# The numerator's state product of a linear-attention layer on half of the contraction rows, in two banks instead of one

## The reference

```python
qkv = x @ W_attn + b_attn                 # 16 heads of 16 channels
q, k = elu(q) + 1, elu(k) + 1
def step(carry, inp):
    kv, ksum = carry                      # per head 16 x 16 and 16
    kv = kv + kt[..., :, None] * vt[..., None, :]
    ksum = ksum + kt
    num = einsum('bhi,bhij->bhj', qt, kv)
    den = einsum('bhi,bhi->bh', qt, ksum)[..., None] + EPS
    return (kv, ksum), num / den
y = y @ W_proj + b_proj
```

## Time and profile before

| | us |
|---|---|
| median of 3 runs | 2399.52 |
| the three runs | 2395.42, 2399.52, 3922.05 |
| profiled execution, its own time | 2388.81 |
| its span, first to last instruction | 2387.1 |
| TensorE busy | 2074.3 |
| VectorE busy | 2055.3 |
| ScalarE busy | 1893.9 |
| GpSimd busy | 1210.0 |

### The profile page before, as it was taken

The page is one execution under the profiler, slowest core; times in us unless marked ns, Lnnn a source line. Parts: engine busy times, 40 slices in busy tenths (PEclk is TensorE's granted clock), DMA queues, the critical chain, the costliest instruction groups (busy, mean ns, idle before and its releaser), DMA issues. The chain is left out here.

```text
span 2387.1 us, 40867 instructions
## 1 busy us (share of the span) xinstructions
PE 2074.3 (87%) x12844; PEld 1296.4 (54%) x12844; DVE 2055.3 (86%) x3876; ACT 1893.9 (79%) x3800; POOL 1210.0 (51%) x1804
## 2 busy tenths in 40 slices
PE   2448898998989899898989989898998989889887
PEld 1115556464655646465565646556564656646574
DVE  7988998979889897989989798998979899897734
ACT  5779887897978789797878979787897978867453
POOL 7114454545545454554546455454645555464744
PEclk8669899999999999999999999999999999999999
DMA  3542422323132232313223232322223132221000
GB/s 84 134 113 54 107 56 66 83 60 92 47 105 56 70 79 63 89 47 104 56 71 79 65 87 50 102 56 75 75 66 85 52 100 56 70 70 34 5 6 12
DMA packets 104452, 165.98 MB, mean 70 GB/s; under 512 B 15459, under 2 KB 34095, under 8 KB 104239
## 3 DMA queue, kind: packets, MB, share of 16 engines
q1 hardware_dynamic: 104238, 163.37, 25.7%
HBM read 146.55 MB, written 16.78 MB: 68 GB/s over the span
## 5 line engine op out<-in xcount | busy, mean ns | idle before, releaser
L1399 DVE TENSOR_TENSOR_SCAN scan_bufs<-scan_bufs,inp_bank 128x512 f32<-128x512 f32 x512 | 617.8, 1207 | 4.9 <-ACT scan_bufs L794 4.4
L1108 PE MATMUL bank<-w_gu,f_xqT 128*128 128x512 f32 x1024 | 496.6, 630 | 36.3 <-ACT f_xqT L857 35.1
L787 ACT ACTIVATE scan_bufs<-scan_bufs,a_rows 128x512 f32<-128x512 f32 x512 | 371.5, 725 | 54.8 <-DMA scan_bufs<-dt_copy 54.5
L1123 PE MATMUL bank<-w_dn,f_hqT 128*128 128x256 f32 x1536 | 357.9, 383 | 8.6 <-ACT f_hqT L857 8.6
L1108 PEld LDWEIGHTS bank<-w_gu,f_xqT 128*128 128x128 f32 x1024 | 201.1, 202 | 269.1 <-issue 265.0
L1409 DVE TENSOR_TENSOR scan_bufs<-scan_bufs,c_bank 128x512 f32<-128x512 f32 x512 | 343.1, 670 | 1.2
L794 ACT ACTIVATE scan_bufs<-scan_bufs 128x512 f32<-128x512 f32 x512 | 323.6, 632 | 3.9
L1123 PEld LDWEIGHTS bank<-w_dn,f_hqT 128*128 128x128 f32 x1536 | 284.3, 190 | 77.3 <-issue 26.0
L688 POOL TENSOR_TENSOR f_h<-f_h,f_h_scale 128x704 f32<-128x704 f32 x128 | 178.1, 1391 | 283.8 <-DVE f_h L1274 283.8
L710 POOL TENSOR_SCALAR_AFFINE_SELECT masked_scores<-masked_scores 128x512 f32<-128x512 f32 x256 | 168.8, 685 | 217.1 <-ACT masked_scores L857 216.8
L699 POOL TENSOR_TENSOR f_h<-f_h,f_h_lean 128x704 f32<-128x704 f32 x128 | 216.1, 1688 | 122.2 <-DVE f_h L1460 113.1
(11 more groups left out here) (196 smaller groups left out, 4408.3 us busy)
## 6 DMA issues: line engine op xcount, KB each, us to landing
scan_bufs<-dt_copy SPq DMA_DIRECT2D x512, 256.0 KB, 4.1
xp<-L_attn_a_x SPq DMA_DIRECT2D x16, 512.0 KB, 4.1
dt_copy<-dt SPq DMA_DIRECT2D x32, 256.0 KB, 2.8
out<-x SPq DMA_DIRECT2D x64, 128.0 KB, 3.5
w_attn<-L_attn_b_W_attn SPq DMA_DIRECT2D x1, 768.0 KB, 4.9
masked_scores<-L_ffn_w_gate SPq DMA_DIRECT2D x1, 704.0 KB
masked_scores<-L_ffn_w_up SPq DMA_DIRECT2D x1, 704.0 KB
f_h<-L_ffn_w_down SPq DMA_DIRECT2D x2, 352.0 KB, 11.1
```

Of the source, the lines that this page charges most:

```text
L787: nc.scalar.activation(half, half, ACT.Exp, scale=a_rows[:, c, at:at + 1]).then_inc(root_ready, 1)
L1108: last = nc.tensor.matmul(to[:, :], f.xqT[:, k, :], w_gu[:, k, g, lo:hi], start=(k == 0), stop=(k == DH - 1))
L1123: last = nc.tensor.matmul(to[:, 0:D], f.hqT[:, k, :], w_dn[:, k, :], start=(k == 0), stop=(k == FK - 1))
L1399: nc.vector.tensor_tensor_scan(half, half, inp[:, :], 0.0, ALU.mult, ALU.add)\
```

## The change

The state product is split by contraction rows. Of a head group of 128 rows the first 64 rows are the four heads of an even set, the last 64 those of an odd set. Each product now uses only the 64 rows of its own heads, of kv and of q. Even and odd products write different banks, uses "num0" and "num1", in each of which only 256 of 512 columns are used (one 128-column piece per head group). The products with the masked scores go to the same places; order and count of all products stay. Each bank gets its own filled signal: num0 after set 2, num1 after set 3. ScalarE copies each with an instruction of its own, 128x256, to sets 0 and 2 or 1 and 3 of numT. a_flip waits for both copies; the exponential of q and k two tiles on waits for num1. VectorE waits for the drain of use "B" before it makes inp. The tables HEAD, LAST_AT and LAST_SHIFT are rewritten as plain lists, GAPS and SHIFT; TIMES and PARTS_AT stay.

```diff
-                  ... "num": ("a_sum", "act", "a_sum"),
+                  ... "num0": ("a_sum", "act", "a_sum"),
+                  "num1": ("a_sum", "act", "a_sum"),
...
 def beat_of(engine, part, step, t, b):
-    at = start_of(engine, part, step, t)
-    if b == NB - 1 and part in LAST_AT:
-        first, gap = LAST_AT[part]
-        at += first - PARTS_AT[part][0] + t * (gap - PARTS_AT[part][1])
-        at += LAST_SHIFT.get(engine, {}).get((part, step), 0.0)
+    at = start_of(engine, part, step, t) + t * GAPS.get((b, part), 0.0)
+    at += SHIFT.get(b, {}).get(engine, {}).get((part, step), 0.0)
...
 (ScalarE, a_root)
-                        wait_drained(act, "R1", b if t > 1 else b - 1, (t - 2) % TILES, "num")
+                        wait_drained(act, "R1", b if t > 1 else b - 1, (t - 2) % TILES, "num1")
 (ScalarE, a_sum)
-                    copy_out(f1, b, t, "num", numT[:, :, :].rearrange("p s n -> p (s n)"), SETS * P)
+                    for e in range(2):
+                        src, done = wait_filled(act, "R1", b, t, f"num{e}")
+                        nc.scalar.activation(numT[:, :, :].rearrange("p (g e) n -> p e g n", e=2)[:, e, :, :],
+                                             src[:, 0:2 * P].rearrange("p (g n) -> p g n", g=DH), ACT.Copy)\
+                            .then_inc(done, 1)
 (TensorE, a_sum)
-                    to, filled = take("R1", b, t, "num", ["v"])
+                    taken = [take("R1", b, t, f"num{e}", ["v"]) for e in range(2)]
                     if t:
-                        for st in range(SETS):
-                            grp, lo = divmod(4 * st, HG)
-                            nc.tensor.matmul(to[:, st * P:(st + 1) * P],
-                                             kv[:, grp, lo:lo + 4, :].rearrange("p h j -> p (h j)"),
-                                             fqk[r][:, 0, grp, :], start=(st == 0), stop=False,
-                                             skip_group_check=True)
+                        for grp in range(DH):
+                            for e in range(2):
+                                rows = slice(RANK * e, RANK * (e + 1))
+                                nc.tensor.matmul(taken[e][0][:, grp * P:(grp + 1) * P],
+                                                 kv[rows, grp, 4 * e:4 * e + 4, :].rearrange("p h j -> p (h j)"),
+                                                 fqk[r][rows, 0, grp, :], start=(grp == 0), stop=False,
+                                                 skip_group_check=True)
                     for st in range(SETS):
+                        grp, e = divmod(st, 2)
                         for j in range(4):
                             head = 4 * st + j
-                            last = nc.tensor.matmul(to[VP * j:VP * (j + 1), st * P:(st + 1) * P], vv[r][:, head, :],
+                            last = nc.tensor.matmul(taken[e][0][VP * j:VP * (j + 1), grp * P:(grp + 1) * P],
+                                                    vv[r][:, head, :], ...
-                    last.then_inc(filled, 1)
+                        if grp == DH - 1:
+                            last.then_inc(taken[e][1], 1)
 (TensorE, a_flip)
-                    to, filled = take("R1", b, t, "numt", ["num"])
+                    to, filled = take("R1", b, t, "numt", ["num0", "num1"])
 (VectorE, inp)
                     src, done = wait_filled(dve, "P", b, 0, "G")
+                    wait_drained(dve, "P", b, 0, "B")
```

More of the change, by code:

```diff
@@ L39 @@
 HEAD_BEAT = 0.6
-def pieces(step, first, gap, which):
-    return [(first + gap * n, "W", i, step) for n, i in enumerate(which)]
 HEAD = {
[L48 to L64, removed]
[5 rows of a table removed]
[L70 to L75, removed]
@@ L76 @@
+    "sp": [
+        (-40, "P", 0, "load"), (1.6, "P", 0, "keep0"), (8.6, "P", 0, "keep1"),
+    ],
+    "dve": [
[16 rows of a table added]
+    ],
+    "pool": [
[6 rows of a table added]
+    ],
+    "act": [
[12 rows of a table added]
+    ],
[6 rows of a table added]
+    ],
 }
 PARTS_AT = {"P": (0, 0, 1), "M": (32, 1, 32), "D": (32, 2, 16), "G": (32, 4, 8), "S": (48.95, 16, 2), "Y": (65.0, 1, 2), "R1": (66, 3, 4), "R2": (95.7, 7, 4)}
-LAST_AT = {"R1": (66, 3), "R2": (94.7, 4)}
-LAST_SHIFT = {
[6 rows of a table removed]
-    },
-    "dve": {
[10 rows of a table removed]
-    },
-    "act": {
[7 rows of a table removed]
-    },
-    "pool": {
[5 rows of a table removed]
-    },
-    "sp": {
-        ("R2", "down"): 9.347,
+GAPS = {(15, 'R2'): -3}
@@ L123 @@
+SHIFT = {
+    15: {
+        "sp": {
+            ("R2", "down"): 8.347,
+        },
[6 rows of a table added]
+        },
+        "act": {
[7 rows of a table added]
+        },
+        "dve": {
[10 rows of a table added]
+        },
+        "pool": {
[5 rows of a table added]
+        },
     },
@@ L189 @@
                   "S0": ("a_s0", "act", "a_s0"), "S1": ("a_s0", "act", "a_s0"), "S2": ("a_s0", "act", "a_s1"),
-                  "S3": ("a_s0", "act", "a_s1"), "kT": ("a_s1", "act", "a_s1"), "num": ("a_sum", "act", "a_sum"),
+                  "S3": ("a_s0", "act", "a_s1"), "kT": ("a_s1", "act", "a_s1"), "num0": ("a_sum", "act", "a_sum"),
+                  "num1": ("a_sum", "act", "a_sum"),
                   "kv": ("a_sum", "dve", "a_sum"), "numt": ("a_flip", "dve", "a_flip"),
@@ L1180, in attention @@
                     pe.wait_ge(s_masked, upto(b, 4 * TILES, 4 * t + 3))
-                    to, filled = take("R1", b, t, "num", ["v"])
+                    taken = [take("R1", b, t, f"num{e}", ["v"]) for e in range(2)]
                     if t:
-                        for st in range(SETS):
-                            grp, lo = divmod(4 * st, HG)
-                            nc.tensor.matmul(to[:, st * P:(st + 1) * P],
-                                             kv[:, grp, lo:lo + 4, :].rearrange("p h j -> p (h j)"),
-                                             fqk[r][:, 0, grp, :], start=(st == 0), stop=False,
-                                             skip_group_check=True)
+                        for grp in range(DH):
[5 more added lines that the diff above has]
+                                                 skip_group_check=True)
                     for st in range(SETS):
+                        grp, e = divmod(st, 2)
                         for j in range(4):
                             head = 4 * st + j
-                            last = nc.tensor.matmul(to[VP * j:VP * (j + 1), st * P:(st + 1) * P], vv[r][:, head, :],
-                                                    sm[r][:, score_at(head), :], start=(t == 0), stop=True,
-                                                    tile_position=(0, VP * j), skip_group_check=True)
-                    last.then_inc(filled, 1)
+                            last = nc.tensor.matmul(taken[e][0][VP * j:VP * (j + 1), grp * P:(grp + 1) * P],
+                                                    vv[r][:, head, :], sm[r][:, score_at(head), :], start=(t == 0),
+                                                    stop=True, tile_position=(0, VP * j), skip_group_check=True)
+                        if grp == DH - 1:
+                            last.then_inc(taken[e][1], 1)
                     if t < TILES - 1:
```

## The result

| | before | after |
|---|---|---|
| median of 7 runs, us | 2395.24 | 2403.84 |
| lowest | 2394.10 | 2403.01 |
| profiled execution, its own time | 2388.81 | 2403.35 |
| span | 2387.1 | 2401.6 |

The measured ratio is 1.0045, interval 1.0035 to 1.0054; the two medians differ by 8.6 us, and by 9.1 us without the one slow run of 3922.05 us among the seven before. The forecast was 2399 us beside 2399.5, no difference: the time lies inside the range, but a slowdown clear of the noise came where none was forecast. Four more runs of the kernel before put its median at 2395.2 instead of the 2399.5 shown earlier, so the comparison "2399 beside 2399.5" hid the slowdown of 3.4 us that is in the sum (2398.8 against 2395.4). The other 5 us or so are missed terms.

What follows compares the result with a forecast made beforehand. No single engine bounds it; TensorE, ScalarE and VectorE alternate on the path. +4.3 us over 14 batches and -0.9 in the last give +3.4: 2392.2 profiled, 2399 us timed beside 2399.5, range 2374 to 2416.

Steps and rivals of the forecast that it cites:

- What bounds: Steady batch: the path alternates between TensorE, ScalarE and VectorE; tiles 2 and 3's numerators lie inside VectorE's stretch, savings there hidden.
- Wait of tile 0's numerator: TensorE, tile 0: num1 gets the bank VectorE drains with L1481, so the burst starts +0.34 us later, in 14 batches.
- Burst of tile 1: TensorE's state product in tile 1: 0.55 us instead of 1.06, saving 0.51 us a batch on the path.
- One more change of the array's shape: TensorE going from 128 rows to 64 before the masked product: priced at 0, bounds 0 and 0.16 us.
- Eight instructions in 0.55 us: State product burst: four pairs at 0.138 us each, priced from the score product, if halves run side by side.
- Flip of tile 1: TensorE's numt in tile 1 waits for the second score copy of tile 2, not the first: +0.48 us, 14 batches.
- Copy and VectorE's wait: ScalarE's split copy, +0.04 us each, and VectorE's wait for B, 71 us of cover: both 0 on the path.
- Sum of a batch: Steady batch: burst -0.51, bank waits +0.34 and +0.48, together +0.31 us; +4.3 us over 14 batches.
- The ends: Last batch, running on latency: three cheaper bursts against two bank waits of about 0.35 us, together -0.9 us.
- The first (saving arrives): Rival: bank waits fall away, a batch gains 0.51 us; timed 2386, or 2373 if all TensorE's saved work counted; chance 0.2.
- The second: Rival: the state product's halves do not overlap, shape change costs 0.16; +0.98 us a batch, timed 2410; chance 0.2.
- The third: Rival: the change does nothing, other waits hide both bank waits and the saving; timed 2395; chance 0.1.

Runs made afterwards that it cites:

- the two kernels with 128 rows in two banks: Changed kernel with state products on all 128 rows, as it is: 2408.91 us, ratio 1.006; with both bank waits planned away: 2396.67 us, 1.001.
- The kernel with the copies first: Changed kernel with both waits planned away and ScalarE's two copies before tile 2's down projection put ahead of an exponential in 13 batches: 2389.40 us, ratio 0.9983.
- the kernel with VectorE's wait: Kernel before with only VectorE's wait for the drain of B added; also called the yardstick: 2395.89 us, ratio 1.0006.
- the five one-bank kernels of the experiments: Kernel before plus numerator wait 1.0015, flip wait 1.0014, both 1.0033, split copy alone 0.9989, VectorE's wait for B alone 1.0006.
- the kernels with the waits added and planned away: Kernel before plus numerator wait, flip wait, both: 1.0015, 1.0014, 1.0033; changed kernel with flip wait, numerator wait, both planned away: 1.0024, 1.0012, 0.9988.

## Why the prediction was wrong

**The two bank waits and the cheaper burst were the right mechanisms; two sizes were off and one loss was not asked for, and all three fell on the same side.** In the order of the prediction's steps:

- *What bounds.* Right. Both added waits came through at nearly their full size, and tiles 2 and 3 gave the period nothing: the 64-row product is worth 0.34 us at best, about the 0.32 of tile 1 alone, which fits that VectorE's stretch hides the others.
- *Wait of tile 0's numerator, forecast +0.34.* Failed in size: +0.54. The drain, 0.29 us behind TensorE's old start, was read rightly (anchored, L1505 ends at the same 8.87 us as L1481 did). The reaction was not: the forecast took 0.05 us from the flip of tile 1 behind its score copy; here it is 0.25 us to the matmul (1062.51 to 1062.76), of which the order of the two waits explains 0.15.
- *Burst of tile 1, forecast -0.51.* Failed in size: -0.32 on TensorE. The halves do overlap: the eight instructions are (0.72 - 0.27) / 7 = 0.064 us apart on average (0.27 is the length of one in this burst), two of them 0.13, against 0.138 forecast; singly, they start in pairs 0.007 us apart, and the pairs follow at 0.21, 0.11 and 0.11 us. Two prices were wrong, that of the change of shape and that of the eight.
- *One more change of the array's shape, forecast 0.* It is 0.09. The first 64-row product starts 0.96 us after the start of the transposes before it, the 128-row one started 0.87 us after them. This is not the second bank wait: the two kernels with 128 rows in two banks have that too, and stand at 0.88. The argument that L1192 followed L1185 without idle was no evidence, as the idle is not drawn between modelled ends; the gap from start to start shows the price. Between products of 128 columns in these rows, the next instruction starts 0.20 to 0.21 us after the last one where the form changes, and about 0.11 where it stays: 1076.98 + 0.45 = 1077.43 to 1077.63 here, 1072.10 - (1071.04 + 0.85) = 0.21 in the kernel before. The prediction's other case, 0.16 us for the change and a saving of 0.35, was nearly the result, and the Trainium skill's rule behind it ("TensorEngine Tiling (Array Packing)", key properties: changing the tiling mode drains the engine) agrees with these gaps.
- *Eight instructions in 0.55 us.* They take 0.65 to the start of the masked product. The price was the mean over the scores' longer burst, and such a mean spreads the fixed part at a change of form over more instructions. In the kernel before, the scores' rows of four start 0.21, then 0.11 us apart, and the next form comes 0.22 us after the start of the last row: four such rows are 0.66 us. So the burst takes 0.65 + 0.09 = 0.74 us, where it took 1.06.
- *What is late next, not asked.* Of the 0.32 some 0.12 was lost at once: the down projection now arrives before ScalarE's f_hqT. The prediction followed each added wait to what stood behind it, but not the saving to what stood before it. The kernel with the copies first shows this loss and its remedy.
- *Flip of tile 1, forecast +0.48.* Right: 0.48 in the timeline, 0.43 in the period when put in alone.
- *Copy and VectorE's wait, forecast 0.* Right, each by a kernel of its own; for the copy it is 0.05 a batch at most.
- *Sum of a batch.* Forecast -0.51 + 0.34 + 0.48 = +0.31. With the measured terms -0.32 + 0.12 + 0.54 + 0.48 = +0.82, measured +0.78 by the period; the rest of 0.04 I have not placed.
- *The ends.* Against the kernel with VectorE's wait, whose span is 2393.4: batch 1 to batch 13 costs 1678.51 - 1670.37 = +8.1 us, the start -2.6 (364.49 against 367.09), what follows batch 13 +2.7 (358.6 against 355.9), together +8.2, near the 8.6 of the timed runs. The last batch was forecast at a gain of 0.9, most of it by 0.7 us from the burst of the earlier trace rows. It did not come. From tile 0 of the last batch on the changed kernel takes 101.1 us and the yardstick 101.2, both at a granted clock of 0.95; the 2.7 us are lost ahead of that, in batches 13 and 14. Without the waits, from batch 13 to the end, it is 354.5 us against 354.7 in the kernel before, both at 0.98 in the last 100 us. Why the start is shorter I did not test: the copy in batch 1 stands between 367.0 and 368.9 us in the five one-bank kernels of the experiments, at 366.2 and 366.5 with 128 rows in two banks, at 364.5 to 365.5 with 64 rows; but the profiled execution of the kernel before, at 363.77, shows that this place also varies by itself.
- *Rivals.* The first (saving arrives) would have needed the waits to fall away; they did only where planned away. The second had the right sign with a reason that is in the main wrong: the halves overlap, and of its 0.16 us for the change of shape 0.09 is borne out. Its +0.98 a batch is also what the two-bank kernel with 128 rows shows, which has the same two waits and no saving; that the rest of it, 0.16 forecast and 0.10 measured, is so near is chance. The third is excluded by the kernels with the waits added and planned away.

## What to carry to other kernels

Where buffers are handed out by a rule in program order, one more use per step re-deals many of them: work out for each use whose drain it now waits for, and put a price of its own on every such wait; here the re-dealing cost 0.9 us a batch and the better product gave 0.2 to 0.34. Break ties of the rule on purpose: two drains planned at one time really stand 0.5 us apart, and a nudge of 0.001 beats was worth 0.39 us a batch. Follow a saving forward as well as a wait: ask which operand the engine now reaches too early, and move the copy that makes it ahead of work that can wait. Price a short burst by its single starts and not by the mean of a longer one.

## What the runs showed of the hardware

- Half the rows did not halve the product: two 64-row instructions on the two halves take 0.13 us on average, against 0.24 for two of 128 rows, but the burst as a whole went only from 1.06 to 0.74 us, since 0.20 us to the next form stays and 0.09 us is lost on the way in. The weight loads show the way in too; timeline of the loads in the kernel after, at that burst. Its first load follows 0.48 us behind the three of the transposes; in the kernel before it was 0.36 and with 128 rows in two banks 0.37.

```profile
1076.50 0.31 PEld L1137 LDWEIGHTS bank<-ident,f_h 128*128 128x128 f32 x3 [0.23 <-DVE fqk L1505]
1076.98 0.52 PEld L1206 LDWEIGHTS bank<-fqk,kv 64*128 64x128 f32 x8 [0.17 <-issue]
1077.63 0.81 PEld L1214 LDWEIGHTS bank<-masked_scores,vv 128*32 128x32 f32 x32
```

- On TensorE a wait that is released last costs 0.22 us from release to the first load when another satisfied wait stood ahead of it, and 0.07 us when it stood first and the satisfied one behind. I had expected the opposite. Two orders in one place, and the wait alone in the kernel before (0.07), are all the evidence; what it comes from stays open.
